# A cross-attention value product on the 128x128 array: odd batches' heads written to the exchanged partition half

## What is computed

```
q = queries @ Wq + bq ; k = keys @ Wk + bk ; v = values @ Wv + bv     (16 heads of 64)
att = softmax(q k^T / 8) over the 64 keys of each head
out = att @ v, heads side by side ; out @ Wo + bo
```

## Time and profile before

| what | before |
|---|---|
| median of 3 runs | 373.63 us (373.61 to 373.88) |
| span of the profiled execution | 370.1 us, 6439 instructions |
| TensorE busy | 319.9 us (86%) |
| VectorE busy | 287.2 us (78%) |
| ScalarE busy | 184.1 us (50%) |
| GpSimd busy | 195.2 us (53%) |
| mean granted TensorE clock | 0.940 |

### The profile page before, as it was taken

The page is one execution under the profiler, slowest core; times in us unless marked ns, Lnnn a source line. Parts: engine busy times, 40 slices in busy tenths (PEclk is TensorE's granted clock), DMA queues, the critical chain, the costliest instruction groups (busy, mean ns, idle before and its releaser), DMA issues.

```text
span 370.1 us, 6439 instructions
## 1 busy us (share of the span) xinstructions
PE 319.9 (86%) x2346; PEld 288.5 (78%) x2346; DVE 287.2 (78%) x659; ACT 184.1 (50%) x357; POOL 195.2 (53%) x247
## 2 busy tenths in 40 slices
PE   8889998899979999999999861116999999999991
PEld 7767886675569999999999851005999999999991
DVE  3898887948888988888888727787588699799850
ACT  2677554555545556775675432362317456652230
POOL 3787889713223468778878766003405515533222
PEclk9999999999999999999999985555999999999998
DMA  7950000000000306306215237001149657612222
GB/s 248 392 192 1 2 0 2 0 0 3 0 2 14 129 29 186 128 16 200 74 70 184 66 121 270 0 1 28 58 127 267 168 193 217 171 16 43 30 30 28
DMA packets 24047, 34.29 MB, mean 93 GB/s; under 512 B 1784, under 2 KB 20560, under 8 KB 23888
## 3 DMA queue, kind: packets, MB, share of 16 engines
q1 hardware_dynamic: 20112, 29.36, 23.7%
q0 software_dynamic: 3072, 4.20, 6.3%
q10 hardware_dynamic: 832, 0.32, 0.4%
HBM read 27.58 MB, written 6.29 MB: 92 GB/s over the span
## 4 chain that ended last, share of the span: by engine, by line
PE 69%; DVE 15%; POOL 7%; ACT 4%; issue 3%; DMA 1%; ACTq 0%; DVEq 0%; POOLq 0%
PE bank L917 12%; PE bank L919 12%; PE bank L918 12%; PE q_banks L917 4%; PE q_banks L918 4%; PE q_banks L919 4%; PE bank L938 4%; DVE flags_all L1271 3%; PE q_banks L718 2%; PE bank L1444 2%; PE bank L736 2%; PE bank L752 2%; PE bank L982 1%; POOL acc L410 1%; DMA X<-in_x 1%
## 5 line engine op out<-in xcount | busy, mean ns | idle before, releaser
L1569 POOL DMA_INDIRECT out_x<-ybuf,idx x16 | 26.3, 1641 | 59.8 <-DVE ybuf L1588 57.7
L1046 POOL TENSOR_TENSOR prob<-prob,rsum 128x1024 f32<-128x1024 f32 x16 | 30.5, 1905 | 18.8 <-DVE rsum L1144 17.3
L917 PE MATMUL bank<-H_hi,PT_hi 128*128 128x256 f32 x128 | 36.3, 284 | 1.7 <-DVE PT_lo L1115 1.7
L917 PE MATMUL bank<-W_hi,h_hi 128*128 128x256 f32 x128 | 37.2, 291 | 0.0
L919 PE MATMUL bank<-H_hi,PT_lo 128*128 128x256 f32 x128 | 36.2, 283 | 0.0
L918 PE MATMUL bank<-H_lo,PT_hi 128*128 128x256 f32 x128 | 36.2, 283 | 0.0
L919 PE MATMUL bank<-W_hi,h_lo 128*128 128x256 f32 x128 | 36.2, 283 | 0.0
L918 PE MATMUL bank<-W_lo,h_hi 128*128 128x256 f32 x128 | 36.2, 283 | 0.0
L1549 POOL DMA_INDIRECT xg<-xn_rows,idx x16 | 18.5, 1158 | 29.5 <-DVE idx L1615 25.3
L1026 ACT ACTIVATE prob<-prob 128x1024 f32<-128x1024 f32 x16 | 16.9, 1059 | 33.5 <-DVE prob L1165 33.4
L1526 ACT ACTIVATE hbuf<-bank,b_cols 128x256 f32<-128x256 f32 x32 | 13.4, 472 | 40.1 <-PE bank L919 40.1
(11 more groups left out here) (269 smaller groups left out, 1063.6 us busy)
## 6 DMA issues: line engine op xcount, KB each, us to landing
W_raw<-in_L_ffn_W SPq DMA_DIRECT2D x16, 1024.0 KB, 5.7
X<-in_x SPq DMA_DIRECT2D x4, 512.0 KB, 6.2
xn_rows<-xn SPq DMA_DIRECT2D x16, 128.0 KB, 1.7
out_x<-X SPq DMA_DIRECT2D x4, 512.0 KB, 3.5
Wq<-in_L_xattn_Wq SPq DMA_DIRECT2D x1, 1024.0 KB, 10.9
Wk<-in_L_xattn_Wk SPq DMA_DIRECT2D x1, 1024.0 KB, 13.8
Wv<-in_L_xattn_Wv SPq DMA_DIRECT2D x1, 1024.0 KB, 15.0
Wo<-in_L_xattn_Wo SPq DMA_DIRECT2D x1, 1024.0 KB, 16.9
```

Source lines behind the costliest of these rows:

```text
L917: t.matmul(out_ps, hi, rhs_hi, start=first, stop=False)
L1046: g.tensor_tensor(prob[:, s], prob[:, s], rsum[:, s].unsqueeze(2).to_broadcast([P, HX, CK]), ALU.mult).then_inc(prob_ready, 1)
L1569: g.indirect_dma_start(out_flat, bass.IndirectOffsetOnAxis(ap=idx[:, e, h:h + 1], axis=0), ybuf[:, h], None, bounds_check=last_row, oob_is ...
```

## The change

Odd batches' products exchange the partition halves of their output: head 0's keys go to partitions 64 to 127, head 1's to 0 to 63 (`head_rows(h ^ b % 2)`), which are the other two quadrants of the array. Bank 0 of a chunk takes the even batches, bank 1 the odd ones, and both banks are waited for ahead of the chunk's first product. The order of the products stays by batch, so bank 0 is full behind the sixth product and bank 1 behind the eighth. H_hi and H_lo are written with the batches `m::2` in place of `2m:2m+2`. So that P meets H's new order, the shifts of odd batches' tiles write the two heads of each pair exchanged (a negative step in the output, L1165); the sums, the exponential and the transposes follow that order by themselves.

```
                 pe.wait_ge(V_ready, c + 1)
-                for m in range(2):
-                    ps = bank_free(f"H{c}{m}")
-                    for b in (2 * m, 2 * m + 1):
-                        for rows in (slice(0, DK), slice(DK, P)):
-                            mm = t.matmul(ps[rows, (b % 2) * D:(b % 2 + 1) * D], V_T[rows, c, b], Wo[rows, c],
-                                          start=True, stop=True)
-                    filled(mm, f"H{c}{m}")
+                ps = [bank_free(f"H{c}{m}") for m in range(2)]
+                for b in range(CB):
+                    for h in range(2):
+                        rows, keys = head_rows(h), head_rows(h ^ b % 2)
+                        mm = t.matmul(ps[b % 2][keys, (b // 2) * D:(b // 2 + 1) * D], V_T[rows, c, b], Wo[rows, c],
+                                      start=True, stop=True)
+                    if b >= CB - 2:
+                        filled(mm, f"H{c}{b % 2}")
...
-                    a.activation(H_hi[:, 2 * m:2 * m + 2, c], v3(ps[:], 2), ACT.Copy).then_inc(H_hi_ready, 1)
+                    a.activation(H_hi[:, m::2, c], v3(ps[:], 2), ACT.Copy).then_inc(H_hi_ready, 1)
...
-                    nc.vector.tensor_tensor(H_lo[:, 2 * m:2 * m + 2, c], v3(ps[:], 2), raw(H_hi[:, 2 * m:2 * m + 2, c]),
+                    nc.vector.tensor_tensor(H_lo[:, m::2, c], v3(ps[:], 2), raw(H_hi[:, m::2, c]),
                                             ALU.subtract).then_inc(H_ready, 1)
...
-                    ins = v.tensor_tensor(prob[:, s, hs], ps, mx[:, s, hs].unsqueeze(2).to_broadcast([P, 8, CK]),
-                                          ALU.subtract)
+                    pairs = lambda ap: ap.rearrange("p (a h) k -> p a h k", h=2)
+                    shifted_to = pairs(prob[:, s, hs])
+                    if new.group % 2:
+                        shifted_to = shifted_to[:, :, ::-1]
+                    ins = v.tensor_tensor(shifted_to, pairs(ps),
+                                          pairs(mx[:, s, hs].unsqueeze(2).to_broadcast([P, 8, CK])), ALU.subtract)
```

More of the change, by code:

```diff
@@ L864, in sc, with head_rows @@
             return [banks[2 * slot], banks[2 * slot + 1]]
+        def head_rows(h):
+            return slice(h * DK, (h + 1) * DK)
         def pe_H(pe):
```

## The result

The changed kernel takes 378.33 us (median of 4 runs, 376.99 to 379.21) against 373.75 (4 runs, 373.61 to 375.89): ratio 1.0122, 95% interval 1.0077 to 1.0167. It is slower by 1.2%, where 373.2 and "same" were forecast and 375.2 was the top of the range. In every run of the record that lists both, the device time is 1.7 to 1.9 us above the span. So the kernel before's profiled execution (span 370.1) stands for some 371.9 us, and of the 3.5 us that the median lay above it about half is that this execution was a quick one. That is why the two spans differ by 6.7 us and the two medians by 4.6.

The account below looks back on a forecast made before the run. TensorE was taken as busy almost throughout, its H work on a chain of waits with VectorE and ScalarE. Terms -1.02 + 0.28 + 0.30 = -0.44 us, with the median's offset to the profile, gave 373.2 us; range 372.8 to 375.2.

Parts of the forecast that it names:

- forecast: Whole kernel: quadrants overlap, clock holds, 0.44 us gained in the stage that makes H; 373.2 us, "same", 43%.
- first rival: Stage making H: quadrants work, but longer TensorE idle gaps drop its clock to half; 373.9 to 374.9 us, 25% chance.
- one fall: Clock drop priced once, at work behind chunk 7's thin stretch (99.5 to 104.4): 1.1 to 1.3 us.
- chunks 0 and 1: nothing: First two chunks of H: TensorE ends 1.5 us sooner, but VectorE's G_lo queue covers it, so no gain.
- bound of 3.9 us for one fall: Highest price of a clock drop: 8 transposes and 12 score matmuls at half speed, from 104.91 on.
- Speed of the products: H's matmuls on four quadrants: a chunk takes 0.86 us instead of 1.72, bank 0 full 1.08 after its start.
- some 2.2 us: Sign that the prediction is right: 32 matmuls of L878 at 80.3 take this long instead of 3.67.
- Chunks 2 and 3: 1.0 gained: Second pair of H's chunks ends earlier, so tile 0's maxima come at 90.87 instead of 91.89: 1.02 us gained.
- 0.28 and 0.30 given back by the up-front waits: Chunks 5 and 7 wait whole for H_lo to free a bank, losing 0.28 and another 0.3 us of the gain.
- Second rival, no overlap: H's quadrants do not overlap, only the up-front waits remain: +1.45 us, 375.1 us, 22% chance.
- Third rival, slow shifts: Reversed shift writes on VectorE are slow, 8 TensorE steps wait 0.2 us or more each: 375 or above, 3% chance.
- strided H_hi and H_lo writes: Writes of H with stride keep the same inner length of 256: no cost.

Follow-up runs that it names:

- e0: The changed kernel measured once more, nothing altered: 377.28 us, ratio 1.0117 against the kernel before.
- e2: The changed kernel with odd batches' shifts written in plain order, so only its time is of use: 377.47 us, ratio 1.0104 against the kernel before.
- e3: The changed kernel plus matmuls nobody reads in TensorE's idle stretches behind chunks 1, 4, 6 and 7: 372.55 us, ratio 0.9998 against the kernel before.
- e7: The changed kernel's layout, but all chunks except 2 and 3 wait for their two banks one after the other: 372.58 us, ratio 0.9988 against before.
- e8: e7 plus matmuls nobody reads behind chunk 1, inside chunks 5 and 7, and behind chunk 7: 370.73 us, ratio 0.9932 against the kernel before.
- e1: The changed kernel with all products on the diagonal quadrants and no reversed shifts, up-front waits kept: 374.33 us, ratio 1.0017 against the kernel before.
- e5: The kernel before with one edit, both banks of a chunk waited for ahead of its first product: 373.97 us, ratio 1.0022 against before.
- e4: The changed kernel plus matmuls nobody reads only behind chunks 6 (4) and 7 (3): 373.99 us, ratio 1.0011 against the kernel before.
- e9: The kernel before plus matmuls nobody reads in its own idle stretches (1, 1 and 3), as a control: 373.46 us, ratio 0.9992 against before.

## Why the prediction was wrong

**The step that failed is the pick between forecast and first rival.** The prediction put 43% on its forecast, in which the quadrants work and the clock holds, and 25% on "The quadrants work, but TensorE's clock falls". It was the latter. It named the mechanism, the idle stretches (2.3, 2.3 and 1.4; measured 2.47, 2.24 and 1.56) and the row that spoke for it. Against it stood that four quadrants are at work in the bursts, and that the clock had stayed full in the stage of before. Neither kept the clock up: all three profiles of kernels with this stage and no fillers (the changed kernel, e0, e2) have three falls, and with fillers (e3) the stage is back within 0.28 us of the forecast.

**The rival's price was mis-sized too.** It counted "one fall" of 1.1 to 1.3 us and named chunk 7's stretch above all. There were three: in the changed kernel's profile they cost 1.0, 1.1 and 2.5, and even a single one of 3.4 us behind that stretch cost 1.5 in e7. The first came behind the stretch that the prediction called free ("chunks 0 and 1: nothing"). That stretch lies under VectorE's queue and costs nothing itself, but what it did to the clock was paid by chunks 2 and 3. The bound of 3.9 us for one fall, had it been used for the top of the range, would have reached 377.1. The three falls' 4.6 us on top of the forecast's 373.2 make 377.8; 378.33 was measured.

**What held, on the same clock:**
- *Speed of the products.* 1.96 for two chunks and 1.09 for one, so 0.87 for each further chunk, forecast 0.86. (The "some 2.2 us" that the prediction named for 32 matmuls is above its own steps: 7 x 0.22 + 0.05 + 0.38 is 1.97.) The bank is full 1.08 after the start: chunk 5 of e3 starts at 96.71 and ScalarE's H_hi at 97.84, 0.05 behind that. Two products in the same row half, in different column halves, run side by side, and in e7 even when two others are queued ahead. The Trainium skill (TensorE: Matmul & The Clock Gate, "The mechanism") says that loads overlap only across row groups and that matmuls begin in program order. The trace does not agree for these 64x64 products: 32 matmuls take 1.96 us, not 3.67, and in e7 four run 0.05 us after the first's start.
- *Chunks 2 and 3: 1.0 gained.* 1.02 in e3, e7 and e8, and none in the changed kernel, where the first fall took it.
- *0.28 and 0.30 given back by the up-front waits.* The total gain of e3 at the transposes is 0.18, forecast 0.44, and the late filler is part of the difference; e7, without those waits, keeps 1.02.
- *Second rival, no overlap.* It did not come true, but e1 tests its price: +1.45 reckoned, +1.80 measured and 374.33 us against 375.1. Part of the nearness is luck: the same way of reckoning gave 0.56 for e5, where 1.57 was measured, because it left out TensorE's own queue behind a whole chunk.
- *Third rival, slow shifts.* 680 ns against 681: nothing. The strided H_hi and H_lo writes cost nothing either: medians of 597 and 680 ns against 597 and 682.

**What lies outside the stage.** The 1.68 us behind the last logits are the clock's as well, but not the change's. While the experts' rows are sorted out, TensorE idles much and the clock is at 0.50 in every profile. The kernels leave that half clock at different times, before at 260.7 and the changed kernel at 270.2. Windows, before and then changed:

```profile
265.00:270.00 5.00, 5.00 (x47) 5.00 (x46) 4.13 (x11) 2.48 (x6) 0.00 (x0) 1.00 0.24 43
```

```profile
265.00:270.00 5.00, 4.99 (x35) 4.85 (x34) 1.62 (x6) 1.43 (x4) 3.42 (x3) 0.50 0.23 70
```

Over all profiles the half clock there lasts 37.6, 41.0 or 44.4 us. With it the way from the last logits (the start of their last matmul) to the first expert's second product takes 46.1 to 46.2, 46.4 to 46.5 and 47.9 to 48.2 us. Changed, e2, e3 and e8 had the longest; before, e1, e4 and e7 the middle one; e0, e5 and e9 the shortest. e0 and the changed kernel's first profile are the same program. A second such thing stands in e3's profile: at 21.6 us, far ahead of the stage, the clock falls for 3.4 us, 16 matmuls take 5.41 us there instead of 3.72, and the first product comes at 82.8. That this lottery, of some 2.0 us at the end and 1.7 at the start, is what spreads the runs of before over 371.8 to 375.9 is likely, not shown.

It also limits what the medians tell. Those of e1, e4 and e5 lie only 0.7, 0.4 and 0.4 us above before's, where the last mark is 1.8, 1.9 and 1.6 later, and e7's lies 1.0 below where its mark is 0.55 later. Why these kernels are some 1.1 to 1.5 us quicker than their stage says is open. The account of the falls therefore rests on the marks and the clock; of the times it uses only that the changed kernel (twice) and e2 stand 3.7 to 4.6 us above before and e3 does not.

## What to carry to other kernels

Making an engine's work quicker in a stage that another engine paces can do worse than gain nothing: on TensorE it opened idle stretches, and what followed them ran at half the clock. Before a matmul stage is sped up, ask which queue is last there, how long TensorE will stand idle, and what stands behind. Where the speed-up pays in one place only, matmuls that nobody reads can fill the rest (e3, e8), and banks that come free at different times are better waited for one by one (e5 against before, e7).

## What was not expected of the hardware

Idle stretches of 2.24 to 2.47 us with some 1 us of matmuls between them were enough for the clock to fall in all three profiles of this stage without fillers, while it stayed full in before's, with stretches of 0.44 to 1.27 us, and in e1's, with up to 1.42. But e7 kept the full clock behind 2.43 us and lost it behind 1.44 and 1.27, so these lengths are no rule. The last fall of the changed kernel lasted 6.8 us, though TensorE was busy 5.59 of the window's 6.90. And the array's quadrants take work out of the program's order: with batches 0, 2, 1, 3 queued, where the first two share their quadrants, four matmuls run 0.05 us after the first's start, and two chunks take 2.01 us against 1.96 in the order 0, 1, 2, 3.
